# A gated residual product over 128 batches on one core: one mask multiplication moved to GpSimd, fewer warm-up products, another order of loads, another place for the last burst, and halves at both ends of the last unit

## The chip, the cores and the metric

The kernel runs on one core of a Trainium2 chip. A core has five engines with queues of their own (TensorE, VectorE, ScalarE, GpSimd, SyncE), a scratch memory of 128 partitions (SBUF), eight accumulator banks of 512 fp32 columns each (PSUM), and 16 DMA engines. The metric is the time of one execution on the device in microseconds, smaller is better.

## The reference

For each of 128 batches `b`, an input `x[b]` of 128 x 512 goes through a linear layer whose weights are mixed for that batch from 8 expert weights, and is added to the result:

```
masked_w = weight * mask[None, :, :]                       # 8 x 512 x 512
w_bot = einsum('bg,got->bot', cond_8, masked_w)            # 128 x 512 x 512
out = x + (einsum('bnt,bot->bno', x, w_bot) + bias)        # 128 x 128 x 512
```

## The kernel before

The 128 batches are cut in 4 windows of 32, the 512 output channels in 2 slices of 256. A slice and a window make a *unit* `u` (8 in all, slice 0 first). In a unit there are 16 *bursts* and 16 *groups*. A burst `b` makes the mixed weights of 16 channels for the unit's 32 batches: 16 matrix products (line 423) into 4 banks, called tiles, from the masked weights `wm`. The tiles are then evicted into `wbot`, tiles 0 and 2 by ScalarE (line 268), tiles 1 and 3 by VectorE (line 328); in the first bursts ScalarE has tile 1 too. In unit 0 the identity is added to the mixed weights with small products (line 406), so x is part of the sum. In later units x is loaded a second time in the layout of the output (`xn`, "output-layout x") into the output buffer `staged`, VectorE adds the bias to it (line 342) and later the sums (line 356). A group is two batches: 8 products of 128 x 256 (line 446) from the transposed x (`xs`, a ring of 10 slots, "ring x") and `wbot` into one bank.

TensorE's order is written out by `PIECES` (the groups, some in halves) and `bursts_before` (which bursts stand ahead of a piece `m`). Bursts run one unit ahead: from the second unit on a pair of bursts of the next unit stands ahead of every second group. The tiles of burst `b` go to a place in `wbot` that group `b % 16` of the unit before has still to read, so `tile_ready` makes an eviction wait for that group (line 165). Banks go round in the order of `TAKEN`; `room` (line 378) makes TensorE wait until what used the bank eight places earlier has been read.

The weights of slice 0 are masked at the start, those of bursts 0, 1, 3 and 7 by VectorE (`BY_VECTOR`), the others by GpSimd (line 193). The masks lie in the ring x's slots until those are needed. The weights of slice 1 are loaded during the units 2 to 4 (`LOAD_W_AT`) and masked by GpSimd.

SyncE issues all loads in one order, and an instruction in it that waits holds up all behind it. ScalarE issues the stores. Seven products of 512 bf16 columns on zeros (`WARM`, line 453) run before the first burst. The last piece (`m == LAST`) is made, added and stored in two parts, one for each batch (lines 358 to 361 and 277 to 280).

Of the kernel before, what the change touches and what calls it, by code (L numbers as in the profile page):

```python
# [10 lines left out]
SL = 256  # L11
SLICES = NO // SL
# [3 lines left out]
GB = 2  # L16
# [18 lines left out]
WARM = 7  # L35
# [8 lines left out]
PIECES += [(_u, _g, 0, CS) for _u in range(1, UNITS) for _g in range(GROUPS)]  # L44
LAST = len(PIECES) - 1

# [23 lines left out]
TAKEN.append((LAST + 1, None))  # L70
# [3 lines left out]
def on_vector(b, j):  # L74

    return j == 3 or j == 1 and b not in BY_VECTOR[:3]

# [10 lines left out]
BY_VECTOR = (0, 1, 3, 7)  # L88
# [11 lines left out]
LAST_UNIT = (WINDOWS - 1) * GROUPS  # L100
LOAD_W_AT = {LAST_UNIT - GROUPS + 14 + _c: _c for _c in range(0, CS, 2)}


def cond_resid_kernel(nc: bass.Bass, x, xn, w, mask, bias, yblk, eye, out):
# [6 lines left out]
    with ctx:  # L111
# [97 lines left out]
        def _(eng):  # L209
# [51 lines left out]

        @block.scalar
        def _(eng):
# [11 lines left out]
            def store_last():  # L275

                for h in range(GB):
                    eng.wait_ge(s_o, LAST + h + 1)
                    eng.dma_start(out[STEPS - 1, :, h * SL:(h + 1) * SL],
                                  staged[:, LAST % OUTB, h * SL:(h + 1) * SL]).then_inc(s_out[LAST % OUTB], 16)  # L280

# [29 lines left out]
            for i in range(OUTB):  # L311
                count = len(range(i, LAST + 1, OUTB)) + (GB - 1 if i == LAST % OUTB else 0)
                eng.wait_ge(s_out[i], 16 * count)
# [9 lines left out]
        def _(eng):  # L323
# [20 lines left out]
            def add_sums(m):  # L344
# [13 lines left out]
                for h in range(GB):  # L358
# [18 lines left out]
        def _(eng):  # L377
# [52 lines left out]

            def piece(m):
                u, g, c, end = PIECES[m]
                n = u * GROUPS + g
                width = (end - c) * CO
                eng.wait_ge(s_x[n % XRING], 16 * (n // XRING + 1))
                if g in (0, SOON):
                    for j in range(TILES):
                        tile_evicted(eng, u * CS + end - 1, j, GROUPS if g else SOON)
                bank = room((m, None))
                for h in range(GB):  # L440
                    if m == LAST and h:
                        bank = room((m + h, None))
                    at_h = 0 if m == LAST else h * width
                    for k in range(KT):
                        at = sums[:, g, c:end, k, h, :] if u % 2 else sums[:, c:end, g, k, h, :]
                        ins = eng.matmul(bank[:, at_h:at_h + width], xs[:, n % XRING, h, k, :], at,  # L446
                                         start=(k == 0), stop=(k == KT - 1))
                    if m == LAST or h == GB - 1:
                        ins.then_inc(s_s2, 1)
# [6 lines left out]
            for m in range(LAST + 1):  # L456
                for b in bursts_before(m):
                    burst(b)
                piece(m)

# [54 lines left out]
```

## Time and profile before

| | us |
|---|---|
| median of 3 runs | 603.08 |
| lowest, highest | 602.42, 604.78 |
| the profiled execution | 604.59 |
| its span | 602.80 |

| engine | busy us | share of the span |
|---|---|---|
| TensorE, products | 592.4 | 98% |
| TensorE, weight loads | 515.1 | 85% |
| VectorE | 320.9 | 53% |
| ScalarE | 142.3 | 24% |
| GpSimd | 36.3 | 6% |

The span runs from the first to the last instruction or transfer of the profiled execution, and 1.79 us of its own time lie around it. An fp32 product appears as two records of TensorE. PEld is its weight loads, which overlap the products. In brackets behind a row of the timeline stands the engine's idle time before it and what ended that; "issue" is a wait that no semaphore explains. The granted clock is the share of full speed that TensorE had.

### The profile page before, as it was taken

The numbers are of one execution on the slowest core, as the hardware profiler recorded it, in microseconds if no ns is written. First come the engines' busy times: TensorE is split into PE (matmuls) and PEld (weight loads), VectorE is DVE, ScalarE is ACT, GpSimd is POOL, SyncE is SP. The second block draws the span as 40 slices with busy tenths as digits, with TensorE's granted clock in tenths as the row PEclk, the third lists the DMA queues.
The fourth block names the chain that finished last, engine by engine and source line by source line (L and its number), as shares of the span: only waits on it lengthen the run. The fifth ranks groups of instructions, "written<-read, shape, count | busy, mean of one in ns | idle before, by whom it ended". The sixth has DMA issues, their size and how long they took to land.

```text
span 602.8 us, 14826 instructions
## 1 busy us (share of the span) xinstructions
PE 592.4 (98%) x6343; PEld 515.1 (85%) x6343; DVE 320.9 (53%) x525; ACT 142.3 (24%) x278; POOL 36.3 (6%) x33
## 2 busy tenths in 40 slices
PE   7899999999999999999999999999999999999998
PEld 5799988888888888888888888888888888888886
DVE  4565445546546556465565565555554654654342
ACT  5343222222222222222222222222222222220000
POOL 3330000000000113231000000000000000000000
PEclk8999999999999999999999999999999999999999
DMA  8976557676776899998766776767767776778852
GB/s 324 406 280 197 199 176 228 235 236 223 230 247 207 295 333 336 352 318 284 247 214 227 251 212 240 233 228 227 241 229 228 237 235 229 225 232 258 296 160 87
DMA packets 60833, 148.33 MB, mean 246 GB/s; under 512 B 6736, under 2 KB 9552, under 8 KB 60768
## 3 DMA queue, kind: packets, MB, share of 16 engines
q1 hardware_dynamic: 40176, 113.00, 58.2%
q10 hardware_dynamic: 20592, 34.39, 15.1%
q8 instruction: 50, 0.82, 0.5%
q14 instruction: 15, 0.12, 0.1%
HBM read 113.81 MB, written 33.55 MB: 244 GB/s over the span
## 4 chain that ended last, share of the span: by engine, by line
PE 94%; DMA 4%; issue 1%; DVE 1%; SPq 0%; POOL 0%; DVEq 0%; POOLq 0%
PE ps L446 73%; PE ps L423 20%; DMA staged<-in_xn 3%; DMA xs<-in_mask 1%; PE ps L406 0%; DVE staged L356 0%; POOL wm L193 0%; SPq L214 0%; DVE wbot L328 0%; DVE wm L193 0%; SPq L229 0%; SPq L220 0%; DVE staged L361 0%; DVE staged L342 0%; DVEq L165 0%
## 5 line engine op out<-in xcount | busy, mean ns | idle before, releaser
L446 PE MATMUL ps<-wbot,xs 128*128 128x256 f32 (+1 forms) x2176 | 459.3, 370 | 1.8 <-DVE wbot L328 1.5
L446 PEld LDWEIGHTS ps<-wbot,xs 128*128 128x128 f32 x2176 | 389.7, 190 | 56.6 <-issue 3.6
L328 DVE COPY wbot<-ps 128x512 f32<-128x512 f32 (+2 forms) x271 | 163.8, 650 | 208.7 <-PE ps L446 181.0
L268 ACT ACTIVATE wbot<-ps 128x512 f32<-128x512 f32 (+2 forms) x277 | 141.1, 568 | 399.4 <-PE ps L423 198.0
L423 PEld LDWEIGHTS ps<-y_sb,wm 32*128 32x128 f32 x4096 | 124.1, 188 | 23.4 <-issue 21.1
L423 PE MATMUL ps<-y_sb,wm 32*128 32x128 f32 x4096 | 137.2, 279 | 3.8 <-DVE wm L193 1.6
L356 DVE TENSOR_TENSOR staged<-ps,staged 128x512 f32<-128x512 f32 x111 | 76.2, 687 | 39.3 <-PE ps L446 39.1
L342 DVE TENSOR_TENSOR staged<-staged,bias_sb 128x512 f32<-128x512 f32 x112 | 78.4, 700 | 11.6 <-DMA staged<-in_xn 11.3
L193 POOL TENSOR_TENSOR wm<-wm,mask_sb 128x512 f32<-128x512 f32 x16 | 20.4, 1298 | 215.5 <-DMA mask_sb<-in_mask 215.5
L356 DVE TENSOR_TENSOR staged<-ps,bias_sb 128x256 f32<-128x256 f32 (+1 forms) x24 | 12.2, 510 | 12.9 <-PE ps L446 10.8
L193 POOL TENSOR_TENSOR wm<-wm,xs 128x512 f32<-128x512 f32 x12 | 15.1, 1270 | 23.0 <-DMA xs<-in_mask 22.9
L193 DVE TENSOR_TENSOR wm<-wm,xs 128x512 f32<-128x512 f32 x4 | 2.7, 686 | 3.9 <-DMA xs<-in_mask 3.9
L453 PE MATMUL ps<-staged 128*128 128x512 bf16 x7 | 3.1, 623 | 1.5 <-DVE staged L363 1.5
L406 PE MATMUL ps<-eye_sb 32*128 32x128 bf16 x64 | 3.7, 220 | 0.5 <-DVE wm L193 0.4
L406 PEld LDWEIGHTS ps<-eye_sb 32*128 32x128 bf16 x64 | 2.0, 97 | 1.7 <-DVE wm L193 0.7
L453 PEld LDWEIGHTS ps<-staged 128*128 128x128 bf16 x7 | 0.9, 140 | 2.8 <-DVE staged L363 1.4
L361 DVE TENSOR_TENSOR staged<-ps,staged 128x256 f32<-128x256 f32 x2 | 0.8, 424 | 2.3 <-PE ps L446 2.3
L268 ACT ACT_TABLE_LOAD x1 | 1.3, 1283 | 3.2 <-issue 3.2
L363 DVE MEMSET staged<- 128x512 f32 x1 | 0.5, 485 | 0.9 <-PEq L473 0.9
L317 POOL MEMSET eye_sb<- 128x576 f32 x1 | 0.6, 579 | 0.3 <-POOLq L473 0.3
L473 POOL MEMSET const-float32-0.0<- 128x1 f32 x1 | 0.1, 99 | 0.2 <-issue 0.2
L473 POOL MEMSET const-bfloat16-1.0<- 128x1 bf16 x1 | 0.1, 102 | 0.0
(2 smaller groups left out, 0.2 us busy)
## 6 DMA issues: line engine op xcount, KB each, us to landing
xs<-in_x SPq DMA_DIRECT2D x128, 512.0 KB, 3.9
out<-staged ACTq DMA_DIRECT2D x119, 256.0 KB, 4.8
staged<-in_xn SPq DMA_DIRECT2D x112, 256.0 KB, 4.3
wm<-in_w SPq DMA_DIRECT2D x12, 512.0 KB, 7.0
mask_sb<-in_mask SPq DMA_DIRECT2D x8, 512.0 KB, 6.5
out<-staged ACTq DMA_DIRECT2D x18, 128.0 KB, 4.0
wm<-in_w SPq DMA_DIRECT2D x8, 256.0 KB, 5.6
xs<-in_mask SPq DMA_DIRECT2D x4, 512.0 KB, 12.8
```

The lines of the kernel that those rows point to most:

```text
L193: return eng.tensor_tensor(wm[:, c, :], wm[:, c, :], by, ALU.mult)
L268: eng.activation(tile_place(b, j, first, end), tile_sums(b, j, first, end), ACT.Copy).then_inc(s_ev_a, 1)
L317: eng.memset(eye_sb[:, :, :].rearrange("p v t -> p (v t)").bitcast(fp32), 0.0).then_inc(s_blank, 1)
L328: eng.tensor_copy(tile_place(b, j, first, end), tile_sums(b, j, first, end)).then_inc(s_ev_v, 1)
L342: eng.tensor_tensor(by_batch(staged_of(m)), by_batch(staged_of(m)), bias_of(m), ALU.add).then_inc(s_xb, 1)
L356: eng.tensor_tensor(at, by_batch(total), at if m >= OWN_X else bias_of(m), ALU.add).then_inc(s_o, 1)
L361: eng.tensor_tensor(at, ps[BANK_OF[m + h, None] % BANKS][:, 0:SL], at, ALU.add).then_inc(s_o, 1)
L363: eng.memset(staged[:, 0, :], 0.0).then_inc(s_zeros, 1)
L406: ins = eng.matmul(bank[j][:, own * P:(own + 1) * P], eye_sb[rows[j], c % (P // CO), :], ones_sb[rows[j], :], start=ahead, stop=behind)
L423: ins = eng.matmul(bank[j][:, k * P:(k + 1) * P], wm[rows[j], c, k * P:(k + 1) * P], y_sb[rows[j], win, :], start=not (ahead and k == own) ...
L446: ins = eng.matmul(bank[:, at_h:at_h + width], xs[:, n % XRING, h, k, :], at, start=(k == 0), stop=(k == KT - 1))
L453: eng.matmul(ps[BANKS - 1][:, :], zeros[:, 0:P], zeros[:, 0:BANK], start=True, stop=True)
```

## The change

1. `WARM` goes from 7 to 4.
2. Burst 7's weights are masked by GpSimd. Tile 1 of burst 3 is evicted by VectorE instead of ScalarE.
3. In SyncE's order the load of output-layout x for piece `m` stands ahead of the load of ring x beside it, and so ahead of the weights and the mask that follow that one.
4. Burst 127, the last, stands ahead of the last group of unit 6 (piece 119) instead of ahead of the first group of unit 7. That first group is now two pieces, over the channels of bursts 112 to 119 and of 120 to 127; its output rows are laid out for that on the host.
5. The last piece is made, added and stored in three parts: the first batch, and two halves of the channels of the second (`ENDING`).

```diff
-WARM = 7
+WARM = 4
...
-PIECES += [(_u, _g, 0, CS) for _u in range(1, UNITS) for _g in range(GROUPS)]
+PIECES += [(_u, _g, 0, CS) for _u in range(1, UNITS - 1) for _g in range(GROUPS)]
+
+FIRST_OF_LAST = len(PIECES)
+PIECES += [(UNITS - 1, 0, 0, HALF), (UNITS - 1, 0, HALF, CS)]
+PIECES += [(UNITS - 1, _g, 0, CS) for _g in range(1, GROUPS)]
 LAST = len(PIECES) - 1
+
+ENDING = ((0, 0, SL), (1, 0, SL // 2), (1, SL // 2, SL))
...
-    return () if n % 2 else tuple(b for b in (n + CS - 1, n + CS) if b < BURSTS)
+
+    if m == FIRST_OF_LAST - 1:
+        return (BURSTS - 1,)
+    return () if n % 2 or m >= FIRST_OF_LAST else (n + CS - 1, n + CS)
...
-    return j == 3 or j == 1 and b not in BY_VECTOR[:3]
+    return j == 3 or j == 1 and b not in BY_VECTOR[:2]
...
-BY_VECTOR = (0, 1, 3, 7)
+BY_VECTOR = (0, 1, 3)
...
+            ahead = OWN_X
             for n in range(XRING, STEPS):
+
+                end = DONE_WITH[divmod(n - XRING, GROUPS)] + X_LEAD + 1
+                for m in range(ahead, end):
+                    load_xn(m)
+                ahead = max(ahead, end)
                 load_x(n)
                 if n in LOAD_W_AT:
                     load_w(1, LOAD_W_AT[n], 2)
-
-                m = DONE_WITH[divmod(n - XRING, GROUPS)] + X_LEAD
-                if m >= OWN_X:
-                    load_xn(m)
-            for m in range(DONE_WITH[divmod(STEPS - 1 - XRING, GROUPS)] + X_LEAD + 1, LAST + 1):
+            for m in range(ahead, LAST + 1):
                 load_xn(m)
...
-                for h in range(GB):
-                    at = staged_of(m)[:, h * SL:(h + 1) * SL]
-                    eng.wait_ge(s_s2, m + h + 1)
-                    eng.tensor_tensor(at, ps[BANK_OF[m + h, None] % BANKS][:, 0:SL], at, ALU.add).then_inc(s_o, 1)
+                for i, (h, o, end) in enumerate(ENDING):
+                    at = staged_of(m)[:, h * SL + o:h * SL + end]
+                    eng.wait_ge(s_s2, m + i + 1)
+                    eng.tensor_tensor(at, ps[BANK_OF[m + i, None] % BANKS][:, 0:end - o], at, ALU.add).then_inc(s_o, 1)
...
+            def group_ready(u, g, end):
+
+                n = u * GROUPS + g
+                eng.wait_ge(s_x[n % XRING], 16 * (n // XRING + 1))
+                if g in (0, SOON):
+                    b = u * CS + end - 1
+                    soon = g == 0 and len(parts_of(b)) > TILES
+                    for j in range(TILES):
+                        tile_evicted(eng, b, j, SOON if soon else GROUPS)
+                return xs[:, n % XRING, :, :, :]
...
+            def last_piece():
+                u, g, _, _ = PIECES[LAST]
+                group = group_ready(u, g, CS)
+                for i, (h, o, end) in enumerate(ENDING):
+                    bank = room((LAST + i, None))
+                    for k in range(KT):
+                        ins = eng.matmul(bank[:, 0:end - o], group[:, h, k, :], sums[:, g, o // CO:end // CO, k, h, :],
+                                         start=(k == 0), stop=(k == KT - 1))
+                    ins.then_inc(s_s2, 1)
```

On TensorE, from the pair of bursts 125 and 126 to the first group of unit 7, before (line 423 is a burst, line 446 a group; `s_ev_a` is raised by ScalarE's evictions, `s_ev_v` by VectorE's, `s_o` by the additions):

```order
L446 MATMUL ps<-wbot,xs 128x256 [waits s_ev_a,s_x0]
L446 MATMUL ps<-wbot,xs 128x256 x7
L446 MATMUL ps<-wbot,xs 128x256 [waits s_ev_v,s_x1]
L446 MATMUL ps<-wbot,xs 128x256 x7
L423 MATMUL ps<-y_sb,wm 128x128 [waits s_ev_a]
L423 MATMUL ps<-y_sb,wm 128x128 [waits s_ev_v]
L423 MATMUL ps<-y_sb,wm 128x128 [waits s_ev_a]
L423 MATMUL ps<-y_sb,wm 128x128 [waits s_ev_v]
L423 MATMUL ps<-y_sb,wm 128x128 x12
L446 MATMUL ps<-wbot,xs 128x256 [waits s_ev_a,s_ev_v,s_x2]
L446 MATMUL ps<-wbot,xs 128x256 x7
```

The same place after the change (line 435 is a burst, line 462 a group):

```order
L462 MATMUL ps<-wbot,xs 128x256 [waits s_ev_a,s_x0]
L462 MATMUL ps<-wbot,xs 128x256 x7
L435 MATMUL ps<-y_sb,wm 128x128 [waits s_ev_v]
L435 MATMUL ps<-y_sb,wm 128x128 [waits s_ev_a]
L435 MATMUL ps<-y_sb,wm 128x128 [waits s_ev_v]
L435 MATMUL ps<-y_sb,wm 128x128 [waits s_ev_a]
L435 MATMUL ps<-y_sb,wm 128x128 x12
L462 MATMUL ps<-wbot,xs 128x256 [waits s_ev_v,s_x1]
L462 MATMUL ps<-wbot,xs 128x256 x7
L462 MATMUL ps<-wbot,xs 128x128 [waits s_ev_a,s_ev_v,s_x2]
L462 MATMUL ps<-wbot,xs 128x128 x7
L462 MATMUL ps<-wbot,xs 128x128 [waits s_ev_a,s_ev_v,s_x2]
```

Burst 127 has moved one group forward, and its fourth tile now takes the bank of tile 0 of burst 126, which ScalarE evicts once the group in front is done; before, its last two tiles took the banks of tiles 0 and 1 of burst 126, a whole group later.

In SyncE's queue, where the weights of slice 1 are loaded, before:

```order
L229 DMA xs<-in_x 128x1024
L214 DMA wm<-in_w 128x1024
L218 DMA mask_sb<-in_mask 128x1024
L234 DMA staged<-in_xn 128x512
L229 DMA xs<-in_x 128x1024
L234 DMA staged<-in_xn 128x512
```

And after:

```order
L244 DMA staged<-in_xn 128x512
L239 DMA xs<-in_x 128x1024
L224 DMA wm<-in_w 128x1024
L228 DMA mask_sb<-in_mask 128x1024
L244 DMA staged<-in_xn 128x512
L239 DMA xs<-in_x 128x1024
```

The load of output-layout x stood behind ring x, the weights and the mask; now it is the first of the four.

## Rows read from the trace of the kernel before

**Rows 1.** The page: span, and busy time of each engine.
```profile
span 602.8 us, 14826 instructions
PE 592.4 (98%) x6343; PEld 515.1 (85%) x6343; DVE 320.9 (53%) x525; ACT 142.3 (24%) x278; POOL 36.3 (6%) x33
```

**Rows 2.** Busy time by stage; the header names the columns.
```profile
core 0: us, PE busy (x) PEld busy (x) DVE busy (x) ACT busy (x) POOL busy (x), PEclk, DMA share, GB/s
6.00:20.30 14.30, 11.56 (x288) 10.17 (x289) 9.62 (x17) 9.71 (x21) 5.08 (x4) 0.88 1.04 395
...
200.00:260.00 60.00, 59.15 (x595) 50.77 (x597) 35.03 (x56) 13.80 (x28) 15.46 (x12) 1.00 0.96 328
```

**Rows 3.** Timeline of TensorE's products at the start: start, length, what, [idle before].
```profile
1.45 3.12 PE L453 MATMUL ps<-staged 128*128 128x512 bf16 x7 [1.45 <-DVE staged L363]
6.14 1.17 PE L423 MATMUL ps<-y_sb,wm 32*128 32x128 f32 x32 [1.57 <-DVE wm L193]
...
14.09 1.17 PE L423 MATMUL ps<-y_sb,wm 32*128 32x128 f32 x30
16.50 1.29 PE L423 MATMUL ps<-y_sb,wm 32*128 32x128 f32 x33 [1.25 <-issue]
...
20.32 3.81 PE L446 MATMUL ps<-wbot,xs 128*128 128x128 f32 x32 [0.77 <-DVE wbot L328]
```

**Rows 4.** Busy time in short stretches, columns as in rows 2.
```profile
8.00:11.00 3.00, 2.90 (x56) 2.61 (x56) 1.69 (x3) 2.76 (x6) 1.58 (x2) 0.50 1.05 393
11.00:11.50 0.50, 0.50 (x24) 0.45 (x24) 0.01 (x1) 0.05 (x1) 0.50 (x1) 0.79 1.04 397
```

**Rows 5.** Timeline of the mask multiplications of slice 0.
```profile
10.67 3.97 POOL L193 TENSOR_TENSOR wm<-wm,xs 128x512 f32<-128x512 f32 x3 [1.42 <-DMA xs<-in_mask]
...
17.63 0.68 DVE L193 TENSOR_TENSOR wm<-wm,xs 128x512 f32<-128x512 f32 x1
...
21.28 2.50 POOL L193 TENSOR_TENSOR wm<-wm,xs 128x512 f32<-128x512 f32 x2 [6.64 <-DMA xs<-in_mask]
```

**Rows 6.** The page's DMA queues: packets, MB, share of 16 engines.
```profile
q8 instruction: 50, 0.82, 0.5%
```

**Rows 7.** Timeline of TensorE's products in the middle.
```profile
204.85 7.17 PE L446 MATMUL ps<-wbot,xs 128*128 128x256 f32 x32
...
214.15 7.17 PE L446 MATMUL ps<-wbot,xs 128*128 128x256 f32 x32
...
224.02 7.17 PE L446 MATMUL ps<-wbot,xs 128*128 128x256 f32 x32
...
242.54 7.17 PE L446 MATMUL ps<-wbot,xs 128*128 128x256 f32 x32
...
251.60 1.15 PE L423 MATMUL ps<-y_sb,wm 32*128 32x128 f32 x26 [0.56 <-DVE staged L356]
252.68 7.17 PE L446 MATMUL ps<-wbot,xs 128*128 128x256 f32 x32
```

**Rows 8.** Timeline of GpSimd and VectorE in the middle.
```profile
217.88 2.50 POOL L193 TENSOR_TENSOR wm<-wm,mask_sb 128x512 f32<-128x512 f32 x2 [7.91 <-DMA mask_sb<-in_mask]
...
219.19 1.74 DVE L342 TENSOR_TENSOR staged<-staged,bias_sb 128x512 f32<-128x512 f32 x1
...
250.25 0.69 DVE L342 TENSOR_TENSOR staged<-staged,bias_sb 128x512 f32<-128x512 f32 x1 [1.40 <-DMA staged<-in_xn]
```

**Rows 9.** Timeline at the start of the last unit.
```profile
539.24 1.08 ACT L268 ACTIVATE wbot<-ps 128x512 f32<-128x512 f32 x2 [3.55 <-PE ps L446]
...
544.47 4.77 PE L446 MATMUL ps<-wbot,xs 128*128 128x256 f32 x21 [0.77 <-DVE wbot L328]
```

**Rows 10.** The chain that ended last: start, length, what.
```profile
9.30 2.07 PE ps L423 x32
...
26.20 3.77 PE ps L446 x32
...
77.17 7.10 PE ps L446 x32
...
86.28 7.10 PE ps L446 x32
```

**Rows 11.** Timeline at the end.
```profile
600.00 0.42 DVE L361 TENSOR_TENSOR staged<-ps,staged 128x256 f32<-128x256 f32 x1 [1.23 <-PE ps L446]
```

More of the change, by code:

```diff
@@ L69 @@
     TAKEN += [(_b, _j) for _b in bursts_before(_m) for _j in range(TILES)] + [(_m, None)]
-TAKEN.append((LAST + 1, None))
+TAKEN += [(LAST + _i, None) for _i in range(1, len(ENDING))]
 BANK_OF = {_key: _i for _i, _key in enumerate(TAKEN)}
 def on_vector(b, j):
-    return j == 3 or j == 1 and b not in BY_VECTOR[:3]
+    return j == 3 or j == 1 and b not in BY_VECTOR[:2]
 def parts_of(b):
@@ L275, in store_last @@
             def store_last():
-                for h in range(GB):
-                    eng.wait_ge(s_o, LAST + h + 1)
-                    eng.dma_start(out[STEPS - 1, :, h * SL:(h + 1) * SL],
-                                  staged[:, LAST % OUTB, h * SL:(h + 1) * SL]).then_inc(s_out[LAST % OUTB], 16)
+                for i, (h, o, end) in enumerate(ENDING):
+                    eng.wait_ge(s_o, LAST + i + 1)
+                    eng.dma_start(out[STEPS - 1, :, h * SL + o:h * SL + end],
+                                  staged[:, LAST % OUTB, h * SL + o:h * SL + end]).then_inc(s_out[LAST % OUTB], 16)
             eng.dma_start(y_sb[:, 0, :], yblk[0]).then_inc(s_y, 16)
@@ L311, in _ @@
             for i in range(OUTB):
-                count = len(range(i, LAST + 1, OUTB)) + (GB - 1 if i == LAST % OUTB else 0)
+                count = len(range(i, LAST + 1, OUTB)) + (len(ENDING) - 1 if i == LAST % OUTB else 0)
                 eng.wait_ge(s_out[i], 16 * count)
@@ L429, in burst @@
                     add_x()
+            def group_ready(u, g, end):
[7 more added lines that the diff above has]
+                return xs[:, n % XRING, :, :, :]
             def piece(m):
                 u, g, c, end = PIECES[m]
-                n = u * GROUPS + g
                 width = (end - c) * CO
[L435 to L438, printed above, removed]
+                group = group_ready(u, g, end)
                 bank = room((m, None))
                 for h in range(GB):
-                    if m == LAST and h:
-                        bank = room((m + h, None))
-                    at_h = 0 if m == LAST else h * width
                     for k in range(KT):
                         at = sums[:, g, c:end, k, h, :] if u % 2 else sums[:, c:end, g, k, h, :]
-                        ins = eng.matmul(bank[:, at_h:at_h + width], xs[:, n % XRING, h, k, :], at,
+                        ins = eng.matmul(bank[:, h * width:(h + 1) * width], group[:, h, k, :], at,
                                          start=(k == 0), stop=(k == KT - 1))
-                    if m == LAST or h == GB - 1:
-                        ins.then_inc(s_s2, 1)
+                ins.then_inc(s_s2, 1)
+            def last_piece():
+                u, g, _, _ = PIECES[LAST]
+                group = group_ready(u, g, CS)
+                for i, (h, o, end) in enumerate(ENDING):
+                    bank = room((LAST + i, None))
+                    for k in range(KT):
+                        ins = eng.matmul(bank[:, 0:end - o], group[:, h, k, :], sums[:, g, o // CO:end // CO, k, h, :],
+                                         start=(k == 0), stop=(k == KT - 1))
+                    ins.then_inc(s_s2, 1)
             eng.wait_ge(s_zeros, 1)
@@ L455, in _ @@
                 burst(b)
-            for m in range(LAST + 1):
+            for m in range(LAST):
                 for b in bursts_before(m):
@@ L459, in _ @@
                 piece(m)
+            last_piece()
 LEAD = {_c: _c if _c < HALF else _c - _c % 2 for _c in range(CS)}
@@ L508 @@
     r = run_bass_kernel_spmd(nc, [arrays], core_ids=[0])
-    got = r.results[0]["out"].reshape(SLICES, NB // GB, NN, GB, SL)
+    got = np.array(r.results[0]["out"])
+    got[n] = got[n].reshape(NN, 2, GB, SL // 2).transpose(0, 2, 1, 3).reshape(NN, GB * SL)
+    got = got.reshape(SLICES, NB // GB, NN, GB, SL)
     full = np.ascontiguousarray(got.transpose(1, 3, 2, 0, 4)).reshape(NB, NN, NO)
```

4 lines of the change are left out of this document (3 added, 1 removed).

## The prediction, made before the changed kernel was run

> **What bounds the kernel now.** I read the page first, then the windows by stage, then the stages in which TensorE was ever idle. TensorE is busy 592.4 us of a span of 602.8 [rows 1]. So only two things can move the time: work put on or taken off TensorE, and its roughly 10 us of gaps. The windows say where these are [rows 2]: 2.74 us are missing between 6.0 and 20.3 us, 0.85 us between 200 and 260 us. Add the 6 us before the first burst, one gap of 0.77 us at 544 us [rows 9] and the tail after the last product at about 600 us. No edit touches the steady part, where a pair of groups and a pair of bursts take 9.11 us (86.28 less 77.17) [rows 10]. The ceiling is therefore a few us, and a measurement of this kernel tells about 0.5%, 3.0 us, from no change.
>
> **The start: three warm-up products fewer, burst 7 masked by GpSimd, one eviction moved.** The seven warm-up products run from 1.45 to 4.57 us, and burst 0 starts at 6.14 us, when VectorE has masked its weights [rows 3]. Three products less (3.12/7 each, 1.34 us together) end earlier in time that is idle anyway: nothing directly.
>
> They have two indirect effects. The first is the clock. 7 products of 512 columns in 3.12 us are 0.45 us each, which is the 1.2 GHz level. Burst 0 (32 records in 1.17 us, from 6.14) ran at 2.4 GHz, as the granted clock of 1.00 says. Then the clock was at 0.50 from 8 to 11 us and was back in the window 11.0 to 11.5 [rows 3, 4]. It rose behind 3.1 us of products and fell behind a gap of 1.57 us. With four products the engine is idle from about 3.2 to 6.14 us, 2.9 us. I take it that burst 0 then runs at 1.2 GHz: a burst takes 2.07 us there against 1.17 us [rows 3, 10]. So burst 2, which started at 9.30 us [rows 10], starts about 1 us later.
>
> The second is the gap of 1.25 us before 16.50 us that no semaphore explains ("issue") [rows 3]. Queue 8 moves 0.82 MB in 50 packets, 16.4 KB each, beside TensorE's 2 x 6343 instructions, so about 256 instructions a packet [rows 6]; I read the gap as TensorE out of instructions while the DMA engines are full (DMA share 1.04) [rows 2]. Before, it fell just ahead of the last product of burst 5: of that burst's 32 records 30 stand before the gap, while 33 stand behind it, one more than burst 6 has [rows 3]. So tile 3 of burst 5 was evicted only behind that, and then VectorE masked burst 7 from 17.63 to 18.31 with TensorE waiting for it [rows 5]. With six instructions fewer ahead of it (three weight loads, three products) a boundary of a fixed count falls behind burst 5. Its evictions then run inside the gap. GpSimd is free at 14.64 (10.67 + 3.97) [rows 5] and needs 1.25 us (2.50 for two), so burst 7 is masked near 16 us if its data are there; at 17.63 VectorE did not wait for them. Then: burst 6 from 16.5 to 17.6, burst 7 to 18.7, its first evictions 0.6 us, group 0 at 19.3 instead of 20.32. That is -1.0 us, and it holds downstream because the next masked bursts are ready in time: GpSimd works on bursts 8 and 9 from 21.28 to 23.78 [rows 5], and TensorE would come to them at 23.1.
>
> The Trainium skill (Runtime: NRT & Kernel Launch, Instruction fetch mechanics) says that instructions come in blocks of 16 KiB, 256 of them, the next one fetched while the current one runs, and that this is mostly hidden. The block size agrees with the row of queue 8; that it is hidden does not hold ahead of 16.50 us here. By its word the gap would not be there and the term would be 0.4 us, the masking alone.
>
> If the request for the next instructions goes out when TensorE has got to a certain place, burst 0 at the low clock moves the gap about 1 us later and eats the gain. So the start lies between -1.0 and +0.1 us; I take -0.4, a little nearer to the lost gain, because the low clock at burst 0 is the likelier. The moved eviction (tile 1 of burst 3 to VectorE) takes about 0.54 us from ScalarE (1.08 for two) [rows 9] and adds as much or a little more to VectorE, ahead of the gap: nothing.
>
> **The middle: output-layout x asked for ahead of ring x.** Between 204.85 and 252.68 us five pairs take 47.83 us where five regular ones take 45.55: 2.28 us too many, of them 0.19 in the pair ended at 214.15, 0.76 in the one ended at 224.02 and 1.03 in the one ended at 252.68 [rows 7, 10]. Here the weights and masks of the second slice of outputs are loaded (DMA share 0.96) [rows 2], and SyncE's queue holds the load of output-layout x behind ring x, weights and a mask that waits for GpSimd. At 250.25 VectorE had waited 1.40 us for that load, and at 251.60 TensorE 0.56 us for VectorE [rows 8, 7]. With the load ahead of those, it waits only for the store that frees its slot. What is queued behind it now, ring x, is wanted ten groups later (some 45 us, at 9.11 a pair), so its delay costs nothing; and TensorE waits for GpSimd nowhere in this stretch, so weights and masks that come 2 us later cost nothing either. This takes off the 1.03 us and the 0.19 us of the first pair.
>
> The rest is another thing. The bias addition at 219.19 took 1.74 us instead of 0.69, while GpSimd multiplied from 217.88 for 2.50 us [rows 8]. It starts at the landing of a mask, not of x. The Trainium skill (SBUF — State Buffer, SBUF: two separate sides) says that a VectorE operation with two SBUF inputs and a GpSimd operation that reads SBUF exclude each other for a whole instruction; the 1.74 us that ends just behind GpSimd's agrees. By that rule masks that now land at other moments may meet other additions. I count 1.2 of 2.28 us, bounds 0 and 2.2.
>
> **Last burst ahead of the group it replaces.** Before, burst 127 stood between groups 15 of unit 6 and 0 of unit 7, and the latter waited 0.77 us for its eviction [rows 9]; with the start of the weight loads I call it 0.9. Now the first half of that group (half of 3.77, 1.9 us, with the channels of bursts 112 to 119) covers this: -0.9 us. Two prices. The first: burst 127's fourth tile needs the bank of tile 0 of burst 126, which ScalarE may only evict when the group just in front is done; before, a whole group lay between. ScalarE takes 0.54 us for it (1.08 for two) once the group is done [rows 9], with some 0.1 us on each side for the signal; three products of 0.04 to 0.06 us cover a bit. So +0.6 us of a new wait, in front of the row of the fourth tile. The second: the group in two halves is 3.77 us (two half groups of unit 0) instead of 3.55 (half of 7.10) [rows 10]: +0.2 us. Sum -0.1, bounds -0.6 and +0.6.
>
> **The end in three parts.** The last four products are cut in halves: 4 of 256 columns are a quarter of 7.10, 1.77 us, 8 of 128 are half of 3.77, 1.89 us: +0.1 us. The last addition takes 0.42 us for 256 columns against 0.69 for 512 [rows 11, 8], so about 0.28 for 128: -0.14. The last store is 64 KB instead of 128; 2.4 us passed from the addition's end at 600.42 to the span's end, and the transfer itself can give 0 to 0.2 us of it. Sum -0.1, bounds -0.3 and +0.2. Rewriting the host layout of one group costs the device nothing.
>
> **Sum.** -0.4 - 1.2 - 0.1 - 0.1 = -1.8 us on the profiled execution's 604.59 us (span 602.80 and 1.79 around it), so 602.8 us. The median of the three runs is 603.08, 1.5 us below the profiled one; applied to it, 601.3 us.
>
> **Rivals.**
> 1. *The masks keep the middle long* (chance 0.22). For it: half of the excess stands beside GpSimd's multiplications, and SyncE now issues weights and mask after a wait for a store. Against it: the longest single wait is plainly for x. The middle gives 0: 603.08 - 0.6 = 602.5 us.
> 2. *Everything opens* (0.15). The gap of missing instructions stays at 16.5 us though burst 0 is slow (the transfer queued among others, not asked for later), and the middle gives 2.2: -1.0 at the start, -2.2 here, -0.3 at the last unit, -0.1 at the end: -3.6, 599.5 us. For it: that gap of 1.25 us can hide about 1 us of delay. Against it: the transfer can hardly be independent of the engine's progress.
> 3. *The clock comes late, slower than before* (0.13). After a start at 1.2 GHz with gaps the full clock is granted only after burst 4 instead of in the window 11.0 to 11.5. Bursts 0, 2, 3 and 4 then cost up to 0.9 us more each: +3.6, less the 1.1 that the gap hides, +2.5; with -1.2 and -0.1 it ends at 604.3 us. It decides if the clock rises later than about 13 us; before that the gap ahead of 16.5 us swallows it. Against it: from 8 to 11 us TensorE was busy 2.90 of 3.00 us even at half clock [rows 4], and will be again.
> 4. The forecast has the rest, 0.50; its own range is 600.3 to 602.5 us.
>
> That the change does not do what it says I exclude: the order of instructions shows all of its moves.
>
> **Numbers.** Faster by over 0.5% means below 600.1: rival 2 nearly whole and a little of the forecast's edge, 0.15. Slower means above 606.1: only rival 3 with a middle that gives nothing (605.5) and a little more besides, 0.04. Within: 0.81. The range 599.8 to 603.9 takes in the forecast, rival 1 and part of rivals 2 and 3.
>
> **What would show it.** Right: burst 0 about 2 us long with a granted clock of 0.5; GpSimd's seventh multiplication ending near 16 us and no VectorE masking at 17.6; group 0 between 19.3 and 20.4 us; hardly any wait of the bias addition for x, pairs of 9.11 to 9.5 us from 205 to 262; a new wait of about 0.6 us inside burst 127 and none before the first half group; the last addition 0.28 us. Wrong: a granted clock of 0.5 beyond 13 us, pairs of 9.8 us or more in the middle, or a gap of instructions at a place where before there was none.

## The result and the profile after

The change made the kernel slower. Over 22 runs of each, the median is 607.17 us (605.14 to 613.29) against 604.64 us for the kernel before (602.42 to 606.74); the ratio is 1.0048, 95% interval 1.0031 to 1.0065. The forecast was 601.3 us in 599.8 to 603.9, 1.8 us below the 603.08 of three runs; measured are 2.5 us above. The profiled execution took 608.26 us, its span is 606.5.

The page after: span, and busy time of each engine [rows 1].

```profile
span 606.5 us, 14878 instructions
PE 594.1 (98%) x6364; PEld 517.9 (85%) x6364; DVE 322.2 (53%) x528; ACT 141.8 (23%) x277; POOL 39.3 (6%) x34
```

The span grew by 3.7 us. I split it at five marks: the start of group 0, the ends of pieces 22, 70 and 118 and the last product's end (the last four from the signals that TensorE raises). From group 0 to piece 22 both traces take 78.74 us. The middle is the time from piece 22 to piece 70 less 218.94 us, which is 24 regular pairs of 9.11 and 0.10 for each of three unit borders.

| | before | after | difference |
|---|---|---|---|
| start of group 0 | 20.32 | 19.88 | -0.44 |
| excess of the middle | 2.20 | 6.51 | +4.31 |
| piece 70 to 118 | 218.96 | 218.96 | 0.00 |
| piece 118 to the last product | 60.82 | 60.98 | +0.16 |
| last product to the span's end | 2.83 | 2.46 | -0.37 |

All of the loss is in the middle. The same windows as [rows 2], after (columns as there):

```profile
6.00:20.30 14.30, 12.22 (x292) 11.26 (x293) 11.06 (x18) 9.64 (x20) 6.60 (x5) 1.00 1.04 396
200.00:260.00 60.00, 58.29 (x580) 49.95 (x579) 32.78 (x52) 13.35 (x27) 15.74 (x12) 0.97 0.90 311
```

TensorE misses 1.71 us there instead of 0.85, and its granted clock has fallen to 0.97. (In the first row the 1.00 says nothing of the time before 10.9 us: the trace's first record of the full clock stands there, and the column takes what lies before a first record as full. Burst 0 shows the level by its length, further down.) Here is the place, in the timeline of the kernel after (TensorE, VectorE, SyncE's and ScalarE's DMA issues, GpSimd); it answers to [rows 7, 8]:

```profile
221.91 0.90 ACTq L285 DMA_DIRECT2D out<-staged  x2
...
230.03 0.33 SPq L244 DMA_DIRECT2D staged<-in_xn  x1
230.41 0.43 SPq L239 DMA_DIRECT2D xs<-in_x  x1
230.88 0.43 SPq L224 DMA_DIRECT2D wm<-in_w  x1
232.19 0.33 SPq L228 DMA_DIRECT2D mask_sb<-in_mask  x1
232.57 0.82 SPq L244 DMA_DIRECT2D staged<-in_xn  x1
...
238.98 0.43 SPq L224 DMA_DIRECT2D wm<-in_w  x1
...
240.35 2.95 POOL L203 TENSOR_TENSOR wm<-wm,mask_sb 128x512 f32<-128x512 f32 x2 [8.18 <-DMA mask_sb<-in_mask]
240.90 1.27 DVE L354 TENSOR_TENSOR staged<-staged,bias_sb 128x512 f32<-128x512 f32 x1 [1.81 <-DMA staged<-in_xn]
...
242.82 1.92 PE L435 MATMUL ps<-y_sb,wm 32*128 32x128 f32 x26 [1.56 <-DVE staged L368]
243.33 0.33 SPq L228 DMA_DIRECT2D mask_sb<-in_mask  x1
243.70 0.45 SPq L244 DMA_DIRECT2D staged<-in_xn  x1
...
244.67 8.03 PE L462 MATMUL ps<-wbot,xs 128*128 128x256 f32 x32
...
281.47 0.69 DVE L354 TENSOR_TENSOR staged<-staged,bias_sb 128x512 f32<-128x512 f32 x1 [2.17 <-DMA staged<-in_xn]
...
282.81 1.15 PE L435 MATMUL ps<-y_sb,wm 32*128 32x128 f32 x26 [1.34 <-DVE staged L368]
```

Read it from the top. In the order there are two loads of output-layout x for each pair of groups, an even and an odd one, and only the even one was moved ahead of the weights and the mask. The two stores of 221.91 free the slots of pieces 54 and 55. SyncE can ask for the x of piece 54 only at 230.03, 8.1 us later, when the first of them has landed. Ring x, weights and mask stand behind it and leave only then; before, ring x and the weights left at 227.77 and 228.14. The load for the odd piece 55 stood behind ring x, weights and mask before the change too, but now they leave in the 2.2 us just ahead of it. It leaves at 232.57 (before: 231.60) into busy DMA engines (DMA share 0.93 from 230.0 to 240.9) and lands at 240.87 (before: 239.26). VectorE waits 1.81 us for it, its addition takes 1.27 us instead of 0.69 beside GpSimd's multiplication, and TensorE stands for 1.56 us. At 282.81 TensorE stands for 1.34 us behind a wait for the odd piece 63, there without GpSimd (the addition takes 0.69 us).

That gap cost a second time. The short windows behind it (last numbers: granted clock, DMA share, GB/s):

```profile
243.00:244.00 1.00, 1.00 (x24) 1.00 (x24) 0.96 (x2) 0.00 (x0) 0.30 (x1) 0.51 1.01 373
244.00:246.00 2.00, 2.00 (x13) 1.60 (x10) 0.00 (x0) 0.00 (x0) 0.00 (x0) 0.50 1.02 309
246.50:248.00 1.50, 1.50 (x8) 1.32 (x7) 0.00 (x0) 0.00 (x0) 0.00 (x0) 1.00 1.02 396
```

Behind a gap of 1.56 us the clock was at its half level from 243.0 to 246.4 us. The 26 records of a burst took 1.92 us instead of 1.15 and two groups 8.03 instead of 7.17 [rows 7]: 1.6 us more. So the pair of pieces that ends at 249.26 took 12.75 us instead of 9.11, of which 1.6 is the clock.

The start, the last unit and the end, against [rows 3, 5, 9, 11]: four warm-up products, burst 0 at half clock, VectorE's masking of burst 3, group 0; then burst 127's wait, and the last addition.

```profile
1.45 1.89 PE L478 MATMUL ps<-staged 128*128 128x512 bf16 x4 [1.45 <-DVE staged L375]
6.08 2.09 PE L435 MATMUL ps<-y_sb,wm 32*128 32x128 f32 x32 [2.74 <-DVE wm L203]
...
10.92 1.78 DVE L203 TENSOR_TENSOR wm<-wm,xs 128x512 f32<-128x512 f32 x1
...
12.77 0.23 PE L418 MATMUL ps<-eye_sb 32*128 32x128 bf16 x4 [1.18 <-ACT wbot L280]
...
15.36 2.23 PE L435 MATMUL ps<-y_sb,wm 32*128 32x128 f32 x63
...
19.88 3.81 PE L462 MATMUL ps<-wbot,xs 128*128 128x128 f32 x32 [0.77 <-DVE wbot L340]
...
543.77 1.15 PE L435 MATMUL ps<-y_sb,wm 32*128 32x128 f32 x26 [0.32 <-ACT wbot L280]
...
604.04 0.29 DVE L373 TENSOR_TENSOR staged<-ps,staged 128x128 f32<-128x128 f32 x1 [0.60 <-PE ps L472]
```

Burst 0 did run at half clock (2.09 us) and burst 7 needs no VectorE any more. There is no gap of missing instructions ahead of burst 6; TensorE now stands at 12.77 instead: VectorE's masking of burst 3, which began at 9.95 before, met GpSimd's, took 1.78 us and ended at 12.70. (The row names ScalarE; that of TensorE's weight load beside it names this masking.) It is not a mark of the new start: e4, with the old one, stands for 1.17 us at the same place.

### The profile page after: what moved, and what is told of

Read it like the earlier page. It is cut to its first block, busy times and chain, and to the rows that moved or that the text cites. A ratio compares the mean times of both kernels' runs of the same rounds, so it can differ in the third digit from the quotient of the medians.

```text
span 606.5 us, 14878 instructions
## 1 busy us (share of the span) xinstructions
PE 594.1 (98%) x6364; PEld 517.9 (85%) x6364; DVE 322.2 (53%) x528; ACT 141.8 (23%) x277; POOL 39.3 (6%) x34
## 4 chain that ended last, share of the span: by engine, by line
PE 88%; DMA 8%; POOL 1%; issue 1%; ACT 1%; SPq 1%; DVE 0%; ACTq 0%; DVEq 0%; POOLq 0%
PE ps L462 68%; PE ps L435 20%; DMA staged<-in_xn 3%; DMA mask_sb<-in_mask 3%; DMA out<-staged 2%; POOL wm L203 1%; DMA xs<-in_mask 1%; PE ps L472 1%; ACT wbot L280 1%; PE ps L418 0%; DVE staged L368 0%; SPq L239 0%; SPq L224 0%; DVE wm L203 0%; SPq L228 0%
## 5 line engine op out<-in xcount | busy, mean ns | idle before, releaser
L435 PEld LDWEIGHTS ps<-y_sb,wm 32*128 32x128 f32 x4096 | 125.7, 190 | 25.7 <-issue 20.5
L435 PE MATMUL ps<-y_sb,wm 32*128 32x128 f32 x4096 | 138.9, 281 | 6.0 <-DVE staged L368 2.9
L368 DVE TENSOR_TENSOR staged<-ps,staged 128x512 f32<-128x512 f32 (+1 forms) x112 | 76.4, 682 | 32.2 <-PE ps L462 32.0
L354 DVE TENSOR_TENSOR staged<-staged,bias_sb 128x512 f32<-128x512 f32 (+1 forms) x113 | 79.2, 701 | 17.8 <-DMA staged<-in_xn 17.7
L203 POOL TENSOR_TENSOR wm<-wm,mask_sb 128x512 f32<-128x512 f32 x16 | 21.9, 1392 | 222.4 <-DMA mask_sb<-in_mask 222.4
L203 POOL TENSOR_TENSOR wm<-wm,xs 128x512 f32<-128x512 f32 x13 | 16.6, 1296 | 21.0 <-DMA xs<-in_mask 20.9
L472 PE MATMUL ps<-wbot,xs 128*128 128x128 f32 (+1 forms) x24 | 3.7, 310 | 0.0
```

What stands on the lines that cost most here:

```text
L203: return eng.tensor_tensor(wm[:, c, :], wm[:, c, :], by, ALU.mult)
L354: eng.tensor_tensor(by_batch(staged_of(m)), by_batch(staged_of(m)), bias_of(m), ALU.add).then_inc(s_xb, 1)
L368: eng.tensor_tensor(at, by_batch(total), at if m >= OWN_X else bias_of(m), ALU.add).then_inc(s_o, 1)
L435: ins = eng.matmul(bank[j][:, k * P:(k + 1) * P], wm[rows[j], c, k * P:(k + 1) * P], y_sb[rows[j], win, :], start=not (ahead and k == own) ...
L472: ins = eng.matmul(bank[:, 0:end - o], group[:, h, k, :], sums[:, g, o // CO:end // CO, k, h, :], start=(k == 0), stop=(k == KT - 1))
```

## The experiments

Each ran beside the kernel before on the same chip. "Excess" is that of the middle as above, and "group 0" its start, both from the one profiled execution of each kernel. One execution says little of small differences: the kernels with the old SyncE order (before, e2, e3, e4) show an excess of 2.20, 0.76, 0.79 and 2.16 us. The three in which the even load alone is first and the loads have their full size (the changed kernel, e1, e9) show 6.51, 4.86 and 3.68.

| kernel | median us (range, runs) | before beside it | ratio, 95% interval | excess | group 0 |
|---|---|---|---|---|---|
| e1, loads' order alone | 607.95 (606.33 to 610.41, 8) | 604.35 | 1.0065 (1.0042, 1.0088) | 4.86 | 20.86 |
| e2, all but the loads' order | 603.29 (602.61 to 604.88, 12) | 604.35 | 0.9988 (0.9974, 1.0003) | 0.76 | 19.93 |
| e3, start alone | 603.97 (603.31 to 604.81, 12) | 604.35 | 0.9996 (0.9981, 1.0011) | 0.79 | 20.16 |
| e4, last unit alone | 604.73 (603.42 to 606.70, 12) | 604.35 | 1.0006 (0.9989, 1.0024) | 2.16 | 20.76 |
| e5, weights last | 602.53 (601.54 to 603.58, 12) | 604.60 | 0.9965 (0.9951, 0.9978) | 0.40 | 20.18 |
| e6, two output-layout x first | 601.79 (601.56 to 602.73, 6) | 604.60 | 0.9951 (0.9934, 0.9969) | 0.14 | 19.61 |
| e8, slice 1's loads slim | 602.11 (601.75 to 602.80, 7) | 604.60 | 0.9953 (0.9938, 0.9967) | 0.03 | 20.16 |
| e9, slice 1's masking short | 605.64 (604.20 to 609.87, 10) | 604.60 | 1.0028 (1.0006, 1.0049) | 3.68 | 19.41 |
| e12, e6's order on before | 602.57 (601.33 to 603.43, 9) | 604.16 | 0.9972 (0.9959, 0.9986) | 0.03 | 20.05 |
| e13, e12 and the start | 602.40 (601.70 to 603.13, 9) | 604.16 | 0.9972 (0.9957, 0.9986) | 0.05 | 19.53 |
| e10, e6 with seven warm-ups | 601.91 (601.59 to 602.58, 5) | 604.16 | 0.9966 (0.9954, 0.9977) | 0.03 | 19.70 |

### Which part of the change costs the time

**e1.** The kernel before with the changed SyncE loop (the diff of part 3) and nothing else.

> The kernel before with one edit: output-layout x ahead of ring x in SyncE's order. Theory 1 (a store holds the head of SyncE's queue): output-layout x of an even piece now waits there for the store two pieces back, which lands some 8 us after its issue while slice 1 is loaded; ring x, weights, mask and then the load for the odd piece stand behind it, leave together, and the odd one lands too late. It expects this edit alone to cost 3 to 5 us (606.5 to 609.5 where before has 604.6), single bias additions that wait 1.5 us or more for odd pieces 53, 55, 63, and one or two gaps of TensorE over 1 us between 225 and 290 us. Theory 2 (the start and the last unit cost the time, the middle's long gap in the one profile is chance) expects the time of before within 0.7 us and pairs of at most 10.2 us.

**e2.** The changed kernel, and in SyncE's loop ring x and weights ahead of output-layout x again:

```diff
             for n in range(XRING, STEPS):
+                load_x(n)
+                if n in LOAD_W_AT:
+                    load_w(1, LOAD_W_AT[n], 2)
 
                 end = DONE_WITH[divmod(n - XRING, GROUPS)] + X_LEAD + 1
                 for m in range(ahead, end):
                     load_xn(m)
                 ahead = max(ahead, end)
-                load_x(n)
-                if n in LOAD_W_AT:
-                    load_w(1, LOAD_W_AT[n], 2)
```

> The changed kernel with SyncE's order as before (ring x, weights and mask, then output-layout x). Theory 1 expects it 2.5 to 4 us below the changed kernel and at or a little below before: 603.0 to 604.8, with the middle's pairs as in the trace of before (excess about 2.3 us). Theory 2 expects it to stay slower than before by 2 us or more.

**e3.** The kernel before with parts 1 and 2 of the change.

```diff
-WARM = 7
+WARM = 4
...
-    return j == 3 or j == 1 and b not in BY_VECTOR[:3]
+    return j == 3 or j == 1 and b not in BY_VECTOR[:2]
...
-BY_VECTOR = (0, 1, 3, 7)
+BY_VECTOR = (0, 1, 3)
```

> The kernel before with four warm-up products, burst 7 masked by GpSimd and tile 1 of burst 3 evicted by VectorE. Both theories expect burst 0 at half clock, group 0 starting 0.3 to 0.6 us earlier than in the trace of before (20.32), and a time 0.2 to 0.7 us below before. If warm-up products fewer cost more than the masking gives, it is at before or above.

**e4.** The kernel before with part 4 of the change; made from the changed kernel with e2's loop and these edits.

```diff
-WARM = 4
+WARM = 7
...
-ENDING = ((0, 0, SL), (1, 0, SL // 2), (1, SL // 2, SL))
+ENDING = ((0, 0, SL), (1, 0, SL))
...
-    return j == 3 or j == 1 and b not in BY_VECTOR[:2]
+    return j == 3 or j == 1 and b not in BY_VECTOR[:3]
...
-BY_VECTOR = (0, 1, 3)
+BY_VECTOR = (0, 1, 3, 7)
```

> The kernel before with burst 127 ahead of piece 119 and the first group of the last unit in halves; the rest as before, the last piece in two parts. Expected: one wait of 0.3 to 0.6 us inside burst 127 for ScalarE's eviction of tile 0 of burst 126, none ahead of the first half group, the two halves 0.2 us longer than one group; time within 0.5 us of before. Theory 2 has 1 us or more of loss here.

The loads' order alone costs 0.65% (3.9 us by that ratio, 3.6 by the medians), a little more than the whole change by the medians, though the two intervals overlap, and without it the changed kernel is at or just below the kernel before. e1's middle shows the same picture: a wait for the odd load, GpSimd beside it, TensorE behind it.

```profile
231.43 1.30 DVE L344 TENSOR_TENSOR staged<-staged,bias_sb 128x512 f32<-128x512 f32 x1 [1.42 <-DMA staged<-in_xn]
...
233.39 1.15 PE L425 MATMUL ps<-y_sb,wm 32*128 32x128 f32 x26 [1.20 <-DVE staged L358]
...
243.31 1.15 PE L425 MATMUL ps<-y_sb,wm 32*128 32x128 f32 x26 [0.34 <-DVE staged L358]
```

Of what I wrote for e1, the time and a gap over 1 us came. The waits are for the odd pieces 53, 55 and 63, as written, but of 1.42, 0.81 and 1.68 us, and the loss is spread over four pairs instead of two long ones. e3 and e4 are within their intervals of no change; group 0 starts only 0.16 us earlier in e3's trace than in that of before, where I had 0.3 to 0.6. In e2 the excess is smaller than the 2.3 us that I expected. In e4 the last unit is 0.1 us longer than before (piece 118 to the last product 60.92 against 60.82), with the wait of 0.3 us in burst 127. Its clock fell once more, from 21.1 to 24.6 us, which no other run showed.

### Why the order costs it: the wait, the neighbours, or GpSimd

**e5.** The changed kernel; weights and mask of slice 1 stand last in the pair.

```diff
             for n in range(XRING, STEPS):
+                load_x(n)
 
                 end = DONE_WITH[divmod(n - XRING, GROUPS)] + X_LEAD + 1
                 for m in range(ahead, end):
                     load_xn(m)
                 ahead = max(ahead, end)
-                load_x(n)
-                if n in LOAD_W_AT:
-                    load_w(1, LOAD_W_AT[n], 2)
+                if n - 1 in LOAD_W_AT:
+                    load_w(1, LOAD_W_AT[n - 1], 2)
```

> The changed kernel with slice 1's weights and mask moved to the end of the pair in SyncE's order: ring x, output-layout x, ring x, output-layout x, then weights and mask. Theory 1 (head of the queue held by a store, and weights and a mask between the even and the odd load of output-layout x) expects no late odd load any more: the middle's excess over regular pairs (6.5 us in the changed kernel, 2.2 in before, from piece 22's end to piece 70's) at 1.2 us or less, and 602 to 603.5 us. Theory 3 (the excess comes from GpSimd's multiplications that exclude bias additions on VectorE) expects an excess of 2 us or more still, as the number of multiplications is the same.

**e6.** The changed kernel; the odd output-layout x joins the even one at the head.

```diff
-                end = DONE_WITH[divmod(n - XRING, GROUPS)] + X_LEAD + 1
+                end = DONE_WITH[divmod(n - XRING, GROUPS)] + X_LEAD + (2 if n % 2 == 0 else 1)
```

> The changed kernel with both output-layout x of a pair ahead of the even ring x, weights and mask. The head of SyncE's queue is held by stores even longer, but nothing of what stands behind is an output-layout x. Theory 1 expects an excess in the middle of 1.5 us or less and 602 to 604 us. If holding the head does harm by itself (loads of ring x or weights that come too late), it is at 606 us or more.

**e8.** The changed kernel with an eighth of the bytes of slice 1's weights and masks; its outputs of slice 1 are not the reference's.

```diff
-                eng.dma_start(wm[:, c:c + count, :], w[s, :, c:c + count, :]).then_inc(s_w[c], 16)
+                k = NT // 8 if s else NT
+                eng.dma_start(wm[:, c:c + count, 0:k], w[s, :, c:c + count, 0:k]).then_inc(s_w[c], 16)
...
-                    eng.dma_start(mask_sb[:, 0:count, :], mask[s, :, c:c + count, :]).then_inc(s_mask[c], 16)
+                    k = k if c else NT
+                    eng.dma_start(mask_sb[:, 0:count, 0:k], mask[s, :, c:c + count, 0:k]).then_inc(s_mask[c], 16)
```

> The changed kernel, but of slice 1's weights and masks only an eighth of each row is loaded (the first mask in full), so the outputs of slice 1 are not the reference's. The multiplications stay as they are. Theory 1 expects the excess of the middle nearly gone (under 1 us) and 601 to 603 us, because stores and loads land fast when the DMA engines are not full. Theory 3 expects 2 us or more of excess still.

**e9.** The changed kernel with GpSimd's multiplications of slice 1 cut to 64 columns; its outputs of slice 1 are not the reference's either.

```diff
-            return eng.tensor_tensor(wm[:, c, :], wm[:, c, :], by, ALU.mult)
+            k = NT // 8 if s else NT
+            return eng.tensor_tensor(wm[:, c, 0:k], wm[:, c, 0:k], by[:, 0:k], ALU.mult)
```

> The changed kernel with all loads, but GpSimd masks only 64 of 512 columns of each row of slice 1 (so slice 1's outputs are not the reference's), which takes its multiplications from 1.25 us to about 0.2. Theory 1 expects waits for odd output-layout x and gaps over 1 us as in the changed kernel, 605 us or more; half a us may go. Theory 3 expects the excess to fall below 1.5 us and the time below 604.

e8 takes away the bytes and keeps the multiplications: the excess is gone (0.03 us). Without the bytes the multiplications moved too and met none of the bias additions (all 0.68 us), so of GpSimd's part only e9 tells. e9 keeps the bytes and shortens the multiplications: the waits for the odd load and the gaps behind them stay. Its GpSimd, VectorE and TensorE:

```profile
239.86 0.60 POOL L204 TENSOR_TENSOR wm<-wm,mask_sb 128x64 f32<-128x64 f32 x2 [12.26 <-DMA mask_sb<-in_mask]
...
240.42 0.69 DVE L355 TENSOR_TENSOR staged<-staged,bias_sb 128x512 f32<-128x512 f32 x1 [2.28 <-DMA staged<-in_xn]
...
241.77 1.15 PE L436 MATMUL ps<-y_sb,wm 32*128 32x128 f32 x26 [1.45 <-DVE staged L369]
```

The bias addition is at its 0.69 us, so GpSimd no longer holds it, and TensorE still stands for 1.45 us. Where VectorE's addition and GpSimd's multiplication met in the changed kernel, that added 0.6 us (1.27 against 0.69) to a wait; it does not make it.

e5 and e6 tell which part of the order does it. In both the odd output-layout x has nothing of slice 1 ahead of it within its pair, and both have almost no excess. In e6 the head of SyncE's queue is held by two stores, and its median is the lowest, just below the 602 to 604 us that I expected. SyncE's queue, VectorE and a pair of bursts in e6, at the place of the long gap:

```profile
225.91 1.21 SPq L244 DMA_DIRECT2D staged<-in_xn  x2
227.16 0.59 SPq L239 DMA_DIRECT2D xs<-in_x  x1
227.80 0.70 SPq L224 DMA_DIRECT2D wm<-in_w  x1
234.49 0.33 SPq L228 DMA_DIRECT2D mask_sb<-in_mask  x1
...
236.63 0.68 DVE L354 TENSOR_TENSOR staged<-staged,bias_sb 128x512 f32<-128x512 f32 x1
237.83 0.68 DVE L354 TENSOR_TENSOR staged<-staged,bias_sb 128x512 f32<-128x512 f32 x1
238.70 2.08 PE L435 MATMUL ps<-y_sb,wm 32*128 32x128 f32 x64
```

No addition waits, and the 64 records of a pair of bursts run through in 2.08 us. The mask's load leaves at 234.49, late, and nobody misses it. TensorE over the same 60 us of e6:

```profile
200.00:260.00 60.00, 59.94 (x656) 51.78 (x655) 34.93 (x57) 14.24 (x28) 13.73 (x12) 1.00 0.93 324
```

The DMA share is 0.93 and the traffic 324 GB/s, as much as in the kernel before (0.96, 328) [rows 2]. The same bytes pass; only their order differs.

How the odd load comes too late can be followed in the traces, from the issue of the store that frees its slot to the landing of the load. All times in us:

| piece, kernel | the store, issue to landing | from there to the load's issue | the load, issue to landing | sum | VectorE's wait |
|---|---|---|---|---|---|
| 55, changed | 9.53 | 0.75 | 8.30 | 18.58 | 1.81 |
| 55, e2 (old order) | 7.39 | 0.54 | 8.90 | 16.83 | 0.08 |
| 55, e6 | 4.51 | 0.02 | 7.77 | 12.30 | 0 |
| 63, changed | 8.80 | 0.47 | 8.67 | 17.94 | 2.17 |
| 63, e2 (old order) | 7.40 | 0.53 | 7.50 | 15.43 | 0 |
| 63, e6 | 9.64 | 0.02 | 5.02 | 14.68 | 0 |

What stands ahead of it in SyncE's queue holds the odd load in these cases for less than 1 us after its store has landed, in the changed kernel hardly longer than in e2. The late part is in the transfers: the store, the load, or both take longer where ring x, weights and mask leave together, just ahead of them. How much of it each of these neighbours makes no run separates. One more wait stands in the same place: the mask's load waits for GpSimd. At 243.33 that had held the queue for 3.9 us behind the weights' load, and the load for piece 57 left 4.0 us after its store had landed. It cost nothing there, since TensorE was late by then (the load landed at 249.25, its addition began at 252.13), but e5 and e6 take this wait away from ahead of the odd load too, so they do not show that it is harmless everywhere.

### The version that beats both, and the start again

**e12.** The kernel before with e6's loop. **e13.** The same with parts 1 and 2 of the change. **e10.** e6 with seven warm-up products (`WARM = 7`).

```diff
+            ahead = OWN_X
             for n in range(XRING, STEPS):
+                end = DONE_WITH[divmod(n - XRING, GROUPS)] + X_LEAD + (2 if n % 2 == 0 else 1)
+                for m in range(ahead, end):
+                    load_xn(m)
+                ahead = max(ahead, end)
                 load_x(n)
                 if n in LOAD_W_AT:
                     load_w(1, LOAD_W_AT[n], 2)
-                m = DONE_WITH[divmod(n - XRING, GROUPS)] + X_LEAD
-                if m >= OWN_X:
-                    load_xn(m)
-            for m in range(DONE_WITH[divmod(STEPS - 1 - XRING, GROUPS)] + X_LEAD + 1, LAST + 1):
+            for m in range(ahead, LAST + 1):
                 load_xn(m)
```

> The kernel before with one edit: in SyncE's order both output-layout x of a pair stand ahead of the even ring x, weights and mask. Theory 1 expects the middle's excess at 0.5 us or less (2.2 in before), so 602 to 603 us, faster than before by 1.5 to 2.5 us. If the changed kernel's other edits carried that run's gain, it is within 0.7 us of before.

> As the last, and four warm-up products, burst 7 masked by GpSimd, tile 1 of burst 3 evicted by VectorE. Expected: group 0 some 0.6 us earlier than in the last, the excess of the middle the same, and 0.3 to 0.8 us faster: 601.5 to 602.5 us.

> The changed kernel with both output-layout x of a pair first and seven warm-up products instead of four. If the number of warm-up products decides when the full clock is granted, it rises before 6 us here and burst 0 takes 1.2 us instead of 2.1, as in the trace of before, and the time is 0.3 us or more below the one with four (601.8). If what decides is when the execution begins and not how many there are, the clock rises anywhere between 4 and 12.5 us, as in the runs with seven and with four so far, and the time is the same within 0.4 us.

The one edit of e12 is faster than the kernel before by 0.28% (1.6 us), and with the whole change around it, in e6, by 0.49% (0.34% in e10, which differs only in its warm-up products). The intervals of e6, e10, e12 and e13 overlap, so how much the other four parts add is not settled by times. Only the profiles give a size: group 0 starts 0.5 us earlier in e13 than in e12, and e13 is 0.2 us faster by its median where I had 0.3 to 0.8.

The warm-up products: e12 has seven and burst 0 at half clock all the same; e10 has seven and burst 0 at full clock. The first burst of e12, then of e10:

```profile
6.07 2.09 PE L425 MATMUL ps<-y_sb,wm 32*128 32x128 f32 x32 [1.45 <-DVE wm L193]
```

```profile
6.33 1.17 PE L435 MATMUL ps<-y_sb,wm 32*128 32x128 f32 x32 [1.70 <-DVE wm L203]
...
16.37 1.29 PE L435 MATMUL ps<-y_sb,wm 32*128 32x128 f32 x33 [1.10 <-issue]
...
19.70 1.47 PE L462 MATMUL ps<-wbot,xs 128*128 128x128 f32 x11 [0.88 <-ACT wbot L280]
```

With seven products the full clock was first granted at 4.4 us (before), 4.7 (e10), 10.7 (e12), 10.9 (e4) and 12.3 (e1); with four between 9.4 and 12.1 in all eight. So seven give an early rise only in some executions, and four gave it in none. Two of five against none of eight would be thin, but the record has the mean granted clock of every execution. A single stretch of 3.4 us at the half level, after the full clock was granted, takes it to 0.997 (half of 3.4 in 603). In the kernels with four warm-up products and little or no excess (e2, e3, e5, e6, e8, e13) it is 0.999 or 1.000 in all 58 executions; in those with seven (e1, e4, e10, e12) it is 0.997 in 15 of 34. Such a stretch can lie elsewhere (in e4's trace it is at 21.1), but most will be the one behind an early rise. What it is worth is small: e10's burst 0 was 0.9 us shorter, its clock fell again from 8.1 to 11.5, the gap of missing instructions came back (1.10 us), and its group 0 starts 0.09 us later than in e6.

## Why the prediction was wrong

**The step that failed** is in the middle: "With the load ahead of those, it waits only for the store that frees its slot", and with it "This takes off the 1.03 us and the 0.19 us of the first pair". Of the two loads of output-layout x in a pair the change moved only the even one ahead of the weights and the mask. The wait of 1.40 us at 250.25 that I priced was for an odd one, piece 57, and so were all waits over 0.05 us for that load in the middle of the trace of before (pieces 49, 51, 53, 57, 61). The odd one has stood behind ring x, weights and mask all along. What is new for it is that those three, 1.5 MB, now wait for the even one's store and leave just ahead of it. So "its delay costs nothing" holds for ring x and fails for what stands behind ring x. The middle gave +4.31 us in the profiled execution where I had -1.2 with bounds of 0 and -2.2. e1 (+3.9 us by its ratio, from this edit alone) shows that the order costs it, and e6 (excess 0.14 with the odd load moved up as well) that the odd load is where it does.

**The wait for the store was not priced at all.** I had it as "only the store that frees its slot". The page of before gives a median of 4.8 us from issue to landing for such stores (4.0 in the page after). The store issued at 221.91 held SyncE until 230.03, 8.1 us. A median over the span hides the stretch with full DMA queues.

**A price was missing altogether:** a gap in the middle can be followed by half clock. It cost 1.6 us in the profiled execution. I had looked at the clock only at the start. Executions of the changed kernel also differ more: their range is 8.2 us against 4.3, and 1.2 us in e6 (of 6 runs). The granted clock of each execution tells part of why: of the 22, five are below 1.000, the profiled one (0.997) and the four longest, 613.29 us (0.992), 610.03, 610.00 and 608.42 (0.997 each). The other 17 have a median of 606.65 us, still 2.0 above the kernel before. So the late loads cost most of the loss without the clock, and the clock makes the long executions.

**The start was right in size and half right in its working.** Group 0 came 0.44 us earlier (I took -0.4). That one pair of traces hits so well is partly luck: with the old start group 0 begins at 20.05 to 20.86 us in four traces (before, e1, e4, e12), with the new one at 19.41 to 20.18 in eight, 0.6 us earlier in the mean. Burst 0 ran at half clock, and GpSimd's masking took VectorE's place. The gap of missing instructions did not move by 1 us with the slow burst 0, as I had it. It shows in seven of the thirteen traces, and TensorE goes on from it at 16.23 to 16.50 us in six of them and at 17.02 in e3, whatever the clock of burst 0 was; in the other six TensorE came to that place at 16.1 us or later and found no gap. The place did move behind burst 5, as I wrote: with seven warm-up products 30 of burst 5's 32 records stand ahead of it, with four all 32. e13:

```profile
14.27 1.17 PE L425 MATMUL ps<-y_sb,wm 32*128 32x128 f32 x32
16.38 1.06 PE L425 MATMUL ps<-y_sb,wm 32*128 32x128 f32 x29 [0.94 <-issue]
```

That supports the reading as missing instructions at a fixed count, and speaks for rival 2's first half (the gap ends at its time though burst 0 is slow), against which I had put that the transfer can hardly be independent of the engine's progress. It stays an inference: no run changed the instructions' transfer. In the changed kernel TensorE came there at 16.4 us, so that the gap took nothing.

**The clock rival (3)** did not happen at the start: the full clock came at 10.9 us, and at 9.4 to 12.3 in the other traces without an early rise, before the 13 us it needed.

**The last unit** came out at +0.1 us (I had -0.1). The removed wait, the new one and the halves were all there; the new wait is 0.32 us on the products' side and 0.51 on the weight loads' instead of 0.6. **The end** gave 0.37 us in the tail and cost 0.06 on TensorE (60.98 against e4's 60.92): -0.3 where I had -0.1. The last addition gave 0.13 of it; from its end to the span's end it is 2.14 us instead of 2.38, 0.18 of that in the smaller last store (1.54 us from issue to landing instead of 1.72).

**Rival 1**, that GpSimd's multiplications keep the middle long, named a real effect of half a us a meeting, but e9 shows that it was not the cause. No rival of mine put a loss in the middle.

## What to carry to other kernels

When a load that has to wait is moved ahead in a queue, everything that it passed now waits with it and leaves in one batch. Look for the next load that is wanted soon and stands behind that batch, and check which load the waits in the trace are for: here it was not the one that moved. Two orders removed nearly all of the excess here with the same traffic: the loads that wait for stores together at the head (0.14 us), or the large ones that nobody waits for last (0.40 us). And price a store's landing by the stretch in which it is waited for, not by its median over the span.

## What the hardware showed that was not expected

- A gap of 1.56 us in an otherwise full TensorE was followed by 3.4 us at half clock (243.0 to 246.4), though TensorE had been at full clock for over 200 us; gaps of 1.20 us in e1, 1.34 us in the changed kernel and 1.45 us in e9 were not.
- When the full clock is first granted varies from 4.4 to 12.3 us between five profiled executions with the same seven warm-up products; with four it was 9.4 to 12.1 in eight.
- A store of 256 KB took 8.1 us from its issue to the release of the load that waits for it, with a DMA share of 0.99 (221.9 to 230.03 us), and the next one 9.5 us.
